# Rows of y in two buffers, the normalised rows made by ScalarE, and the image keys copied earlier

## What is computed

```python
def _L0_cond_ref(x, image, mask, ...):        # causal attention, 16 heads, one image key and value in front
    q, k, v = split(x @ c_attn_w + c_attn_b)
    k = concat([image @ uk_w.T + uk_b, k]); v = concat([image @ uv_w.T + uv_b, v])
    attn = softmax(where(causal, q @ k.T / 4, -10000) + mask)
    return (attn @ v) @ c_proj_w + c_proj_b                        # y

def _L0_attn_ref(y, ...):                     # linear attention on y, then a layer norm
    q, k, v = relu(y @ Wq.T + bq), relu(y @ Wk.T + bk), y @ Wv.T + bv
    kv = einsum('bnhd,bnhp->bhdp', k, v)
    denom = maximum(einsum('bnhd,bhd->bnh', q, k.sum(1)), 1e-6)
    r = einsum('bnhd,bhdp->bnhp', q, kv) / denom + y
    return (r - r.mean()) / sqrt(r.var() + 1e-5) * gamma + beta

x = x + _L0_attn_ref(_L0_cond_ref(x, ...))
x = x + fp4_ffn(lstm(x))                      # an LSTM over the sequence, then an FFN with FP4 rounding
```

## Time and profile before

| | us |
|---|---|
| median of 3 runs | 989.18 |
| the profiled execution, its own time | 991.4 |
| its span, first to last instruction | 989.6 |

### The profile page before, as it was taken

How to read it: one execution, slowest core, us unless ns; L and a number is a source line. 1 busy time by engine, 2 the same in 40 slices (tenths; PEclk the granted TensorE clock), 3 DMA queues, 4 the chain that set the end, 5 groups by cost and what they waited for, 6 DMA issues and landing times.

```text
span 989.6 us, 22961 instructions
## 1 busy us (share of the span) xinstructions
PE 809.4 (82%) x7750; PEld 502.5 (51%) x7750; DVE 759.8 (77%) x1836; ACT 420.5 (42%) x1081; POOL 369.0 (37%) x500
## 2 busy tenths in 40 slices
PE   3336777788888888888777999999999999999984
PEld 2123444455555455555454556665566655666542
DVE  5167878787878788888653788888888888888884
ACT  2144535455555555555433343333433334333331
POOL 0034766766767677677630111111111111111111
PEclk9657867798999899999889999999999999999998
DMA  5955445566666666666510000000000000000001
GB/s 118 196 137 98 98 95 108 100 137 128 131 139 132 133 125 142 130 141 134 95 29 22 1 22 23 20 15 22 22 23 17 17 23 22 23 19 14 23 23 27
DMA packets 192752, 72.28 MB, mean 73 GB/s; under 512 B 163633, under 2 KB 191665, under 8 KB 192692
## 3 DMA queue, kind: packets, MB, share of 16 engines
q1 hardware_dynamic: 192692, 71.45, 34.5%
HBM read 25.19 MB, written 8.47 MB: 34 GB/s over the span
## 4 chain that ended last, share of the span: by engine, by line
PE 32%; DVE 9%; issue 6%; ACT 4%; POOL 1%; DVEq 0%; DMA 0%; POOLq 0%; ACTq 0%; SPq 0%
PE bank L906 8%; PE bank L895 6%; PE bank L990 6%; PE bank L758 6%; DVE hqT L1520 3%; PE bank L982 3%; ACT hqT L1191 2%; DVE h_value L170 1%; PE bank L886 1%; DVE bank L164 1%; ACT sig L1156 1%; DVE ffn_room L1486 1%; DVE bank L166 0%; DVE fc L1454 0%; DVE h L1470 0%
## 5 line engine op out<-in xcount | busy, mean ns | idle before, releaser
L710 POOL TENSOR_TENSOR ffn_room<-h_value,h_scale 128x704 f32<-128x704 f32 x32 | 44.4, 1387 | 292.4 <-DVE h_value L171 292.4
L758 PE MATMUL bank<-gu,xqT 128*128 128x512 f16 (+1 forms) x576 | 129.2, 364 | 1.0 <-DVE xqT L1535 1.0
L906 PE MATMUL bank<-wh,h 128*64 128x512 f16 x768 | 100.2, 385 | 3.5 <-ACT h L1166 2.1
L895 PE MATMUL bank<-wx,x1T 128*64 128x512 f16 x768 | 95.3, 384 | 3.8 <-DMA x1T<-x_split 3.8
L636 POOL TENSOR_TENSOR prob<-prob,row_max 128x520 f32<-128x520 f32 x64 | 69.0, 1077 | 48.0 <-DVE row_max L1337 47.9
L895 PEld LDWEIGHTS bank<-wx,x1T 128*64 128x64 f16 x768 | 78.8, 202 | 15.8 <-DMA x1T<-x_split 4.3
L990 PE MATMUL bank<-dn,hqT 128*128 128x256 f16 x576 | 70.1, 277 | 20.5 <-DVE hqT L1520 20.5
L758 PEld LDWEIGHTS bank<-gu,xqT 128*128 128x128 f16 x576 | 54.0, 98 | 53.8 <-issue 10.6
L1156 ACT ACTIVATE sig<-bank 128x256 f32<-128x256 f32 x64 | 24.7, 387 | 130.1 <-PE bank L906 126.7
L643 POOL TENSOR_TENSOR p<-prob,p 128x512 f16<-128x512 f32 x64 | 71.7, 1121 | 12.4 <-ACT p L1074 11.9
L758 PE MATMUL bank<-attn,xT 128*128 128x512 f16 x192 | 73.9, 545 | 0.0
(11 more groups left out here) (193 smaller groups left out, 1892.8 us busy)
## 6 DMA issues: line engine op xcount, KB each, us to landing
vimg_in<-image_values SPq DMA_DIRECT2D x32, 136.0 KB, 3.1
x_in<-in_x_columns SPq DMA_DIRECT2D x16, 256.0 KB, 2.6
x_res<-in_x SPq DMA_DIRECT2D x16, 256.0 KB, 3.0
x_rows<-x_rows_sb SPq DMA_DIRECT2D x32, 128.0 KB, 1.8
ffn_room<-x_rows SPq DMA_DIRECT2D x64, 64.0 KB, 2.2
out<-ffn_room SPq DMA_DIRECT2D x64, 64.0 KB, 2.0
add_mask<-in_mask_Bx1x1xS_ff SPq DMA_DIRECT2D x2, 512.0 KB, 7.5
qkT<-qk SPq DMA_TRANSPOSE x64, 4.1
```

The lines of the kernel that those rows point to most:

```text
L710: pool.tensor_tensor(blocks(hq, FF), blocks(fp4_h.value, FF), spread(fp4_h.scale, FF), ALU.mult).then_inc(s["hq_ready"], 1)
L758: last = pe.matmul(dst, lhs(a, c), rhs(b, c), start=first and c == 0 and a == b, stop=c == C - 1 and (a, b) == parts3[-1], skip_group_chec ...
L895: last = pe.matmul(bank[e][B * h:B * h + B, :], x1T16[m][:, c, :, at], half_cols(wx16, a, c, h), start=False, stop=True, skip_group_check= ...
L906: last = pe.matmul(bank[e][B * h:B * h + B, :], h16[:, m, c, :], half_cols(wh16, a, c, h), start=False, stop=True, skip_group_check=True)
```

## The change

`y_rows` becomes two buffers, one for even and one for odd tiles; ACT's wait for the residual then looks two tiles back. z is computed by ACT as `Identity(rstd * res + offset)`, with offset = -mean * rstd, a new instruction of one column on DVE in the place where DVE computed z; ACT's new instruction stands between the high part of x and the copy of query and key. POOL's copy of the image keys moves from behind `probs_lo(t2, 1)` to ahead of `shift(t2, 1)`. The value and magnet areas of `fp4_h`, which had room of their own, lie in `prob` and `qk16`, which the second stage doesn't use otherwise.

```diff
-    y_rows = sb("y_rows", [P, D])
+    y_rows = sb("y_rows", [P, 2, D])
+    offset = sb("offset", [P, 1])
-    fp4_h = Fp4(sb, "h", FF, small=(wide[:, 2 * FF:2 * FF + FF // BLK], wide[:, 2 * FF + FF // BLK:2 * FF + 2 * FF // BLK]))
+    fp4_h = Fp4(sb, "h", FF, (prob[:, :, :].rearrange("p h k -> p (h k)")[:, 0:FF],
+                              qk16[:, :, :, :].rearrange("p h s d -> p (h s d)").bitcast(BF16)[:, 0:FF]), small=(wide[:, 2 * FF:2 * FF + FF // BLK], wide[:, 2 * FF + FF // BLK:2 * FF + 2 * FF // BLK]))
...
+            if t1:
+                after(pool, s["scores_ps"], t1.count(2, 2, back=1))
+                pool.tensor_copy(qkT[:, :, H // 2:H, S:KEYS].rearrange("p b g o -> p g (b o)"),
+                                 kimgT[:, :, bass.ds(t1.number() * 2, 2)]).then_inc(s["kimg_in"], 1)
             if t2:
                 shift(t2, 1)
                 probs_lo(t2, 0)
                 image_part(t2, 1)
                 probs_lo(t2, 1)
-            if t1:
-
-                after(pool, s["scores_ps"], t1.count(2, 2, back=1))
-                pool.tensor_copy(qkT[:, :, H // 2:H, S:KEYS].rearrange("p b g o -> p g (b o)"),
-                                 kimgT[:, :, bass.ds(t1.number() * 2, 2)]).then_inc(s["kimg_in"], 1)
...
-                pool.tensor_tensor(res_rows[:, :], ctx_rows[:, :], y_rows[:, :], ALU.add).then_inc(s["resid"], 1)
+                pool.tensor_tensor(res_rows[:, :], ctx_rows[:, :], y_rows[:, t4.parity, :], ALU.add).then_inc(s["resid"], 1)
...
                 x_hi(Tile(t1.loop, t1.b + 1))
+            if t5:
+                act.wait_ge(s["offset_ready"], t5.count())
+                after(act, s["zg_ready"], t5.count(back=1))
+                act.activation(z_rows[:, :], res_rows[:, :], ACT.Identity, bias=offset[:, 0:1], scale=rstd[:, 0:1])\
+                    .then_inc(s["z_ready"], 1)
...
-                after(act, s["resid"], t3.count(back=1))
+                after(act, s["resid"], t3.count(back=2))
                 after(act, s["yT_ps"], t3.count(back=1))
-                act.activation(y_rows[:, :], bank[6][:, 0:D], ACT.Copy, scale=1.0 / W_P).then_inc(s["y_sb"], 1)
+                act.activation(y_rows[:, t3.parity, :], bank[6][:, 0:D], ACT.Copy, scale=1.0 / W_P).then_inc(s["y_sb"], 1)
...
                 dve.wait_ge(s["rstd_ready"], t5.count())
-                after(dve, s["zg_ready"], t5.count(back=1))
-                dve.tensor_scalar(z_rows[:, :], res_rows[:, :], mean_var[:, 0:1], rstd[:, 0:1], ALU.subtract, ALU.mult)\
-                    .then_inc(s["z_ready"], 1)
+                after(dve, s["z_ready"], t5.count(back=1))
+                dve.scalar_tensor_tensor(out=offset[:, :], in0=mean_var[:, 0:1], scalar=-1.0, in1=rstd[:, :],
+                                         op0=ALU.mult, op1=ALU.mult).then_inc(s["offset_ready"], 1)
```

More of the change, by code:

```diff
@@ L331, in program @@
         kv_ps kv_masked ctx_ps den_ready den_inv ctx_div resid stats_ready mean_ready var_ready
-        rstd_ready z_ready zg_ready xb_ready x1_ready x1_hi x1_lo x1T_in
+        rstd_ready offset_ready z_ready zg_ready xb_ready x1_ready x1_hi x1_lo x1T_in
         gates_ps sig_if sig_o tanh_g i_g cell_ready tanh_c h_ready h_hi h_lo
@@ L943, in step @@
             if t3:
-                rows_transpose(t3, bank[6][:, D:2 * D], y_rows, "y_sb", "yT_ps")
+                rows_transpose(t3, bank[6][:, D:2 * D], y_rows[:, t3.parity, :], "y_sb", "yT_ps")
             ffn_transpose(t4, "mean")
```

## The result

The changed kernel takes 993.59 us (median of 14 runs, 991.22 to 999.51), the kernel before 990.5 us on the same chip (median of 14 runs). The ratio of the means, without one execution of the kernel before that took 1170.44 us, is 1.0046, with a 95% interval of 1.0026 to 1.0066: slower by 3.1 us in the medians and 4.5 in the means, where 968 us had been forecast with a range of 957 to 983. The execution that was profiled took 994.2 us, with a span of 992.5 us.

The account below looks back on a forecast made before the run. The loop from residual over y_rows, bn_aggr and rstd to the next residual was taken to bound the kernel. Gains of 12.5 (steady), 6.3 (chores) and 2.6 (last steps), less 0.4, made 21.0 us: 968 us forecast, range 957 to 983.

Parts of the forecast that it names:

- What bounds the kernel: First stage: closed loop from residual over y_rows, bn_aggr, rstd and POOL's list to the next residual, 12.77 us a period.
- Two buffers of y: First stage: y_rows no longer waits for the residual; bn_aggr at +0.96 instead of +1.83, 0.87 us less.
- z on ACT: Offset on DVE 0.17, done at +2.36; z starts on ACT at +2.44; copy of query and key at about +2.9.
- rival "slower": Table loads before z and before exp, 1.28 us each, on the loop: period 14.7, total 1049 us; chance 0.06.
- Periods of 13: Sign of being wrong: such periods remain in the steady part, where 12.0 to 12.3 us from y_rows to y_rows was expected.
- z itself: Length of z's ACTIVATE on ACT: 0.46 to 0.62 us, taken as 0.54.
- From the copy to the next residual: Copy of query and key to exp 1.75 us, image_part at +5.53, then 6.61 to the next residual's end.
- the walk: Step-by-step timing of one full-clock period of the changed first stage, residual to residual: 12.14 us.
- Half clock moves elsewhere: Rival: PE idles before the outer products, half the periods keep 0.7 us; period 12.5, total 978 us; chance 0.18.
- Image keys at nothing: POOL's 0.25 us copy of image keys moves ahead of shift(t2, 1): bounds -0.25 to +0.25, taken as 0.
- Chores and last steps: Seven steps with chores gain 6.3 us; last three steps gain 2.6, less 0.4 for the last tile.
- Better than the sum: Rival: PE's work moves ahead, half clock goes everywhere, loop closes at about 11.8 us; total 957 us; chance 0.10.

Follow-up runs that it names:

- the kernel with the cheap offset: The changed kernel with offset made by a tensor_scalar, one tensor input and rstd as scalar, instead of the form reading two tensors: 962.49 us, ratio 0.9713.

## Why the prediction was wrong, step by step

**What bounds the kernel** was read rightly. The closed loop from residual over y_rows and `bn_aggr` to the next residual was there, and freeing y breaks it: 32 us with the buffer alone. The second branch, over PE's wait for y and the lower clock behind it, was there too; PE's wait fell from 32.8 to 3.0 us.

**Two buffers of y.** `bn_aggr` was put at +0.96 and came at +0.83. Right.

**z on ACT: the step that failed** is one term of the sum, the length of `offset`. The path behind it was right: z waits for `offset`, and the copy of query and key, exp and `image_part` stand behind z. The working took 0.17 for `offset` because "it has one column", "as for `bn_aggr`: done at +2.36". The offset measured 1.00 and was done at +3.02. The term was sized by the number of columns and by an instruction beside which POOL stands idle (`bn_aggr`, for which POOL waits), and it was given one value and no upper bound. Yet the same paragraph had the row that says otherwise: z on DVE, which stood at this very place, took 1.14 us beside POOL's shift and 0.41 where POOL was idle. In the kernel before z ended 0.15 us behind the shift's end in every tile that had a shift beside it; `offset` ends within 0.02 us of it. The shift sets the end in both, though one has 256 columns and the other one. `offset` begins with the shift, since the one waits for `rstd` and the other follows it in POOL's list. With bounds of 0.17 and 1.1 the copy of query and key would have come at +2.9 to +3.8, and the upper end was no better than the kernel before in its half-clock periods (+3.81). It came at +3.64, near that end. The rival "slower" had put the turn at 0.63 us more a period ahead of exp, and tied it to table loads; exp came 0.72 later than worked out (+5.37 against +4.65), by the offset alone, and half clock added to it. Periods of 13, named as a sign of being wrong, are the mean of the steady part.

The Trainium skill (SBUF — State Buffer, Who interferes with whom) says that a VectorE instruction with two SBUF inputs contends with a GpSimd instruction that reads SBUF, that one with at most one SBUF input, outside certain fast modes, doesn't, and that the order of issue decides which of two is blocked. The trace agrees: the shift started 0.16 us ahead, and the offset behind it took 1.00 us with two inputs, in either form, and 0.21 with one. This rule spoke against the change, and the prediction didn't weigh it.

**z itself** was put at 0.46 to 0.62, taken as 0.54, and measured 0.60. No table loads were added: the trace has two, as before. The Trainium skill (ScalarE: Activation LUTs, What ACT_TABLE_LOAD costs) made this an estimate of 0.59, with which the trace agrees better than with the value taken.

**From the copy to the next residual.** 1.75 to exp and 0.88 to `image_part` measured 1.73 and 0.88; the remaining 6.61 measured 6.46. With one term put right, the walk is nearly right: the kernel with the cheap offset has 12.16 us where 12.14 was worked out, and takes 962.5 us, inside the range that was given for the change. That the two agree to 0.02 is partly luck: most of its periods alternate between 11.83 and some 12.4 us, and in the one shown above the copy comes at +2.69, 0.2 ahead of the +2.9 worked out. But the walk has z at the head of ACT's step throughout, and the runs put a price on that place as well: 7.7 us more with the cheap offset.

**Half clock moves elsewhere** was a rival with a chance of 0.18, at 978 us; its place, before the outer products, was named rightly, and the clock did fall behind it. But it wasn't an independent case: with the cheap offset, and so the shorter walk, it is nearly gone (0.99), and with the slow one it cost 0.56 us in the mean of all steady periods on top of the walk.

**Image keys at nothing:** right to some 4 us. Both pairs of kernels have the moved copy faster, by 2.9 and 3.5 us in the medians, which these runs show only weakly.

**Chores and last steps:** 6.3 and 2.2 us of gain were forecast, 3.9 and 5.3 measured; the two misses nearly cancel, which is luck. So the whole miss, 23.8 us on the profiled executions, is nearly that of the steady periods: 11.0 lost where 12.5 were to be gained.

**"Better than the sum"** at 957 us, with a period of 11.8, was set aside because "z on ACT still follows `rstd`". That objection was right for z at the head of ACT's step, and it points at the flaw of the change. Without z on ACT the kernel is at 957.3 and 953.7 us, with 11.83 and 11.82 us a period. z on VectorE still takes 1.13 to 1.14 us there, in the median, but ACT's copies don't wait for it or for `rstd`. With z on ACT behind the copies it is at 954.8 us: z still follows `rstd`, and the copies no longer follow z.

**Behind the last y_rows** lie 1.9 us more: from its start to the span's end it is 482.5 us before and 484.4 after. The traces split it. The last residual ends 0.43 later, counted from that start; offset and z then take 0.37 more, where the prediction had 0.4; and 1.1 is in the second stage, which lasts 469.1 us in this execution and 467.9 to 468.4 in all the others, so nothing shows that this share is the change's.

## What to carry to other kernels

Before sizing a small VectorE instruction by its columns, look at what GpSimd runs at that moment and count the tensors that the instruction reads from SBUF: where an operand is one column wide, the form that takes it as a scalar costs 0.21 us here and the form that takes it as a second tensor costs whatever is left of GpSimd's instruction. One tensor is not enough for every instruction: z on VectorE reads one of 256 columns beside its two scalars, and stood for the shift as well (1.14 us against 0.41). No run here tells what sets the two apart. When an instruction is moved to another engine, its place in that engine's list matters as much as its length: an instruction that waits for a late input goes behind those whose inputs are there (7.7 us, or 34 us with the slow offset, for moving z down by some lines). And in a change of several parts, ask of each part what it would give alone; here one part gave 32 us and the other took 29 by itself and 39 beside the first.

## What the runs showed of the hardware

A one-column product on VectorE lasted 1.005 us in the middle of 32, six times its shortest 0.159 us; in each of the 29 tiles where a GpSimd instruction of 1.05 to 1.17 us had started 0.07 to 0.17 us ahead of it, it ended within 0.02 us of that one's end. The form with one tensor took 0.21 us beside the same instruction. And adding 1.25 us of matmuls in a place where TensorE waited made the kernel 12 us faster, with the granted clock at 1.00 instead of 0.91.
